# Projection of q, k and v from fp16 high and low parts in three products, with the modulation products moved in between the first row tiles

## The chip, the cores and the metric

One core of one Trainium2 chip runs the whole program. The time is the device time of one execution in microseconds (us). The engines are TensorE (PE, its weight loads PEld), VectorE (DVE), ScalarE (ACT), GpSimd (POOL) and SyncE (SP), which here only issues DMAs.

## The reference

The program is one transformer block on `x` of shape (2, 2048, 256): conditioned layer norm, attention of 16 heads, conditioned layer norm, a mixture of 8 experts. The change touches only the first part, which for each of the B = 2 batches is:

```python
mod = (silu(c) @ wmod).reshape(B, 6, 1, 256)      # rows sa, ca, ga, sb, cb, gb
ga = (2 * (ga >= 0) - 1) * max(abs(ga), 0.25)     # gb likewise
h = layernorm(x) * (1 + ca) + sa
Q, K, V = h @ Wq.T + bq, h @ Wk.T + bk, h @ Wv.T + bv
query_norms = norm(Q)                             # per row and head; the top 409 queries attend
```

## The kernel before

Two blocks of code matter, `setup_block` (L147) and `project_block` (L289). All engines run their own instruction stream and meet through semaphores; the blocks are divided by a barrier, and after the projection comes `select_block`, which starts when the rows of q and k have been written to memory.

**Setup.** Scale `1 + ca` is folded into the weights and shift `sa` into the biases. PE transposes Wq, Wv and Wk (L238), ACT copies each out of PSUM (`wt`, L209), DVE multiplies by `ca1` into `wtb` in fp32 (L280), PE computes the bias rows (L254, after two of the three copies), DVE adds them (L284).

**Projection.** There are 32 tiles of 128 rows in 8 groups of four (`BLK`); each engine runs an unrolled list of stages. In step s it runs stage number n on tile s - n, so the place in the list is the lag, and the order in the list is the order on that engine:

- DVE: `norm` (lag 0, L385, with the statistics `stats` L369 and L373 of the next group after the second tile of a group and `invert` L378 after the fourth), `evacuate` (lag 4, L396 and L397: q and v out of PSUM with their bias), `squares` (lag 5, L401), `modulation` (lag 6, L410 to L423: nine instructions in nine consecutive steps, the first for tile 5, that turn the rows `ga` and `gb` into clipped ones).
- PE: `turn_h` (lag 1, L544, two fp32 transposes), `project` (lag 3, L552, q and v at once: two fp32 products with 512 columns), `project_k` (lag 4, once in four tiles, L562: K transposed, four fp32 products with 512 columns).
- ACT: `copy_ht` (lag 2, L488, and once in a group `deviation` L482), `first` (lag 4, L495 and L497), `second` (lag 5, L501), `first_k` (lag 6, once in a group, L516 and L518 for two halves), `second_k` (lag 8, once in a group, L530).
- POOL: `second` (lag 5, L456), `third` (lag 6, L460), `second_k` (lag 7, L468), `third_k` (lag 9, L473). q and k are stored as three bf16 parts; these lines compute the rests.
- SP issues the saves of q and k (L350, L342).

An fp32 product shows in the trace as two matrix instructions, so `project` is x4 and `project_k` x8. A tile number t is passed through PSUM buffers `p_h` and `p_qv` with two copies each; `turn_h(t)` waits until the copy of tile t - 2 is out. Ahead of the first tile PE multiplies the four pieces of the modulation rows (L571, 16 matrix instructions), which ACT copies out (L535) before it does anything for a tile.

Of the kernel before, what the change touches and what calls it, by code (L numbers as in the profile page):

```python
# [16 lines left out]
F32 = mybir.dt.float32  # L17
# [8 lines left out]
P = 128  # L26
# [129 lines left out]
def setup_block(nc, ctx, io, cst):  # L156

    with ExitStack() as own:
# [19 lines left out]
        s_ps, s_done, satb_done, wt_ps, wt_done, wtb_done = sem("s_ps"), sem("s_done"), sem("satb_done"), sem("wt_ps"), sem("wt_done"), sem("wtb_done")  # L178
        bias_ps, bk_ps, bias_done = sem("bias_ps"), sem("bk_ps"), sem("bias_done")
# [4 lines left out]
        with nc.Block() as block:  # L184
# [13 lines left out]
            def _(act):  # L198
# [64 lines left out]
            def _(dve):  # L263
# [8 lines left out]
                dve.tensor_scalar(ca1[:, :, :], p_s[:, 1, :, :], 1.0, None, ALU.add).then_inc(s_done, 1)  # L272
# [3 lines left out]
                for i in range(3):  # L276
                    dve.wait_ge(wt_done, i + 1)
# [11 lines left out]
def project_block(nc, ctx, io, cst):  # L289

    with ExitStack() as own:
        sb, ps, sem = places(nc, own, "project")
        R, BLK = 4, 4
        NB = NT // BLK
# [5 lines left out]
        ht = [sb(f"ht{i}", [P, KD, BLK, P], F32) for i in range(2)]  # L300
# [15 lines left out]
        h_done, h_ps, ht_done = sem("h_done"), sem("h_ps"), sem("ht_done")  # L316
# [27 lines left out]
        with nc.Block() as block:  # L344
# [19 lines left out]
            def _(dve):  # L364
# [11 lines left out]
                def invert(j):  # L376
                    dve.wait_ge(sd_done, j + 1)
                    dve.reciprocal(rstd[j % 2][:, :], sd[j % 2][:, :]).then_inc(rstd_done, 1)  # L378

                def norm(t):  # L380

                    j, i = divmod(t, BLK)
                    wait(dve, h_ps, t - R + 1)
                    dve.wait_ge(rstd_done, j + 1)
                    dve.tensor_scalar(h[t % R][:, :], x[:, t, :], mv[j % 2][:, i, 0:1], rstd[j % 2][:, i:i + 1], ALU.subtract, ALU.mult).then_inc(h_done, 1)  # L385
                    if i == 1 and j + 1 < NB:
                        stats(j + 1)
                    if i == 3 and j + 1 < NB:
                        invert(j + 1)

                def evacuate(t):
# [4 lines left out]
                    dve.tensor_tensor(y[t % R][:, :], p_qv[t % 2][:, 0:D], biasb[:, b, 0:D], ALU.add).then_inc(y_done, 1)  # L396
                    dve.tensor_tensor(cst["v"][:, t % TPB, b, :], p_qv[t % 2][:, D:2 * D], biasb[:, b, D:2 * D], ALU.add).then_inc(v_done, 1)  # L397
# [6 lines left out]
                FIX = 5  # L404
# [22 lines left out]
                unrolled([norm, None, None, None, evacuate, squares, modulation])  # L427

                def last_keys():
# [3 lines left out]
                    dve.tensor_scalar(yk[1][:, :], p_k[1][:, :], bkb[:, 1, B - 1:B], None, ALU.add).then_inc(last_y[1], 1)  # L433
                    dve.wait_ge(k_saved[(NB - 1) % 2], 16 * KD * PARTS * ((NB - 1) // 2))
                    dve.tensor_scalar(k3[(NB - 1) % 2][1][:, 0, :], p_k[1][:, :], bkb[:, 1, B - 1:B], None, ALU.add).then_inc(last_first[1], 1)
# [42 lines left out]
            def _(act):  # L478
# [4 lines left out]

                def copy_ht(t):
# [3 lines left out]
                    act.activation(ht[t // BLK % 2][:, :, t % BLK, :], p_h[t % 2][:, 0:D].rearrange("p (k n) -> p k n", k=KD), ACT.Copy).then_inc(ht_done, 1)  # L488
# [3 lines left out]
                def first(t):  # L492
                    act.wait_ge(y_done, t + 1)
# [9 lines left out]
                def first_k(j):  # L503

                    b = j * BLK // TPB
                    if j == NB - 1:
                        act.wait_ge(k_ps, KD * j + 1)
                        act.wait_ge(krest_done, KD * (j - 1) + 1)
                        act.activation(yk[0][:, :], p_k[0][:, :], ACT.Identity, bias=bkb[:, 0, b:b + 1]).then_inc(last_y[0], 1)
                        act.wait_ge(k_saved[j % 2], 16 * KD * PARTS * (j // 2))  # L510
                        act.activation(k3[j % 2][0][:, 0, :], p_k[0][:, :], ACT.Identity, bias=bkb[:, 0, b:b + 1]).then_inc(last_first[0], 1)
# [1458 lines left out]
```

## Time and profile before

| what | value |
|---|---|
| three runs | 1243.06, 1241.56, 1240.20 us (median 1241.56) |
| the profiled execution's own time | 1228.09 us |
| its span in the trace | 1226.3 us |
| busy over the span: PE, DVE, ACT, POOL | 1008.8, 900.4, 646.7, 621.6 us |
| setup | 0 to 19.5 us |
| projection | 19.5 to 128.7 us, next block's first work at 135.0 us |

The profile is of one execution. Its times count from the start of the span. Busy is the time in which an engine runs an instruction of its own; the granted clock of PE is given as a share of full speed, 1.00 for 2.4 GHz and 0.50 for 1.2 GHz. Everything behind the projection (selection, attention, routing, experts) is the same in both kernels.

### The profile page before, as it was taken

The page shows a single profiled execution, that of the slowest core. Times are in us where ns is not written, and L with a number is a line of the kernel's source. Part 1 is how long each engine was busy: PE and PEld are TensorE (multiplying, and loading weights), DVE is VectorE, ACT ScalarE, POOL GpSimd, SP SyncE. Part 2 cuts the span into 40 slices and gives each one's busy share as a digit, 9 for nine tenths or more (in the row PEclk, how much of TensorE's full clock was granted, in tenths as well). Part 3 has the DMA queues.
Part 4 walks back from the last instruction along what each step waited for, and adds up shares of the span by engine and source line. Part 5 has one row for each costly group of instructions (what it writes and reads, how often), then busy time and mean ns, then how long its engine had stood idle before and what let it go on. Part 6 is the DMA issues. An engine that isn't in the chain of part 4 may idle for free. (4 is left out here: it accounts for less than half of the span.)

```text
span 1226.3 us, 29092 instructions
## 1 busy us (share of the span) xinstructions
PE 1008.8 (82%) x7725; PEld 616.7 (50%) x7726; DVE 900.4 (73%) x2189; ACT 646.7 (53%) x1448; POOL 621.6 (51%) x649
## 2 busy tenths in 40 slices
PE   7999002399999999999996776169999999999995
PEld 4444001133333333333333665157778888888884
DVE  4885689788777777777773887937778777777774
ACT  2778196067666666666674453335454444444441
POOL 1688382435554545554436986024554455444543
PEclk9999555589999999989998787579999999999998
DMA  6244771211111111111104895089994232223322
GB/s 222 104 148 153 258 221 60 59 28 37 33 46 31 32 44 33 44 32 32 44 4 130 251 272 172 1 213 216 232 228 79 48 52 43 47 47 52 52 43 27
DMA packets 129163, 118.69 MB, mean 97 GB/s; under 512 B 18064, under 2 KB 117072, under 8 KB 129104
## 3 DMA queue, kind: packets, MB, share of 16 engines
q1 hardware_dynamic: 106840, 95.02, 26.6%
q0 software_dynamic: 20480, 21.53, 11.0%
q10 hardware_dynamic: 1784, 1.44, 0.4%
q8 instruction: 26, 0.43, 0.2%
q14 instruction: 33, 0.27, 0.1%
HBM read 57.27 MB, written 37.60 MB: 77 GB/s over the span
## 5 line engine op out<-in xcount | busy, mean ns | idle before, releaser
L961 DVE TENSOR_REDUCE attend_mxh<-attend_p_a 128x1 f32<-128x512 f32 x416 | 266.3, 686 | 89.3 <-PE attend_p_a L1092 66.5
L1031 ACT ACTIVATE w<-attend_p_b 128x409 f32<-128x409 f32 x480 | 227.5, 514 | 128.3 <-PE attend_p_b L1108 112.4
L1832 ACT ACTIVATE expert_hr<-expert_p,b1t 128x256 f32<-128x256 f32 (+1 forms) x376 | 134.3, 423 | 192.7 <-PE expert_p L1770 138.0
L1725 POOL DMA_INDIRECT out_x<-expert_ys,expert_drop x72 | 122.3, 1699 | 190.7 <-DVE expert_ys L1867 133.5
L1108 PE MATMUL attend_p_b<-attend_qt,w 98*128 98x409 bf16 x480 | 166.9, 352 | 1.6 <-issue 1.3
L1092 PE MATMUL attend_p_a<-w,attend_qt 96*128 96x512 bf16 x384 | 153.4, 403 | 6.7 <-ACT attend_qt L1022 2.2
L905 POOL DMA_INDIRECT attn_d<-outs,idx x93 | 91.0, 978 | 118.9 <-DVE attend_mxh L961 112.5
L1792 PE MATMUL expert_p<-w,expert_hhi 128*128 x800 | 136.7, 273 | 0.6 <-DVE expert_ys L1867 0.2
L1770 PE MATMUL expert_p<-expert_xhi,w 128*128 128x256 f16 x800 | 136.3, 273 | 0.0
L886 POOL DMA_INDIRECT attend_qsel<-q_d,idx x96 | 92.2, 960 | 85.0 <-DVE attend_mxh L961 64.8
L1118 PE MATMUL attend_p_o<-w,attend_vh 128*32 128x409 f32 x1024 | 119.6, 540 | 5.9 <-ACT w L1031 3.1
L1715 POOL DMA_INDIRECT expert_xs<-h_d,expert_take x72 | 73.4, 1019 | 75.7 <-DVE expert_take L1871 54.7
L1792 PE MATMUL expert_p<-w,expert_hlo 128*128 x400 | 109.0, 273 | 0.0
L1108 PEld LDWEIGHTS attend_p_b<-attend_qt,w 98*128 98x128 bf16 x480 | 46.5, 98 | 118.6 <-ACT w L1031 79.4
L1892 DVE TENSOR_TENSOR expert_hlo<-expert_hr,expert_hhi 128x512 f16<-128x512 f32 x144 | 100.5, 698 | 5.0
L1890 DVE CAST expert_hhi<-expert_hr 128x512 f16<-128x512 f32 x144 | 62.4, 433 | 47.1 <-ACT expert_hr L1832 45.5
L1792 PEld LDWEIGHTS expert_p<-w,expert_hhi 128*128 128x128 f16 x800 | 78.2, 98 | 13.2 <-issue 3.7
L1770 PEld LDWEIGHTS expert_p<-expert_xhi,w 128*128 x800 | 78.3, 98 | 9.2
L1770 PE MATMUL expert_p<-expert_xlo,w 128*128 128x256 f16 x400 | 76.3, 273 | 0.0
L1770 PE MATMUL expert_p<-expert_xhi,expert_wu 128*128 128x128 f16 x704 | 68.2, 223 | 1.4 <-DVE expert_xlo L1875 1.4
L1787 PE MATMUL expert_p<-w,expert_hhi 128*128 x176 | 60.9, 380 | 3.1 <-issue 1.6
L1092 PEld LDWEIGHTS attend_p_a<-w,attend_qt 96*128 96x128 bf16 x384 | 38.0, 100 | 47.2 <-DVE attend_mxh L961 14.9
(352 smaller groups left out, 1955.9 us busy)
## 6 DMA issues: line engine op xcount, KB each, us to landing
expert_wu<-w SPq DMA_DIRECT2D x88, 256.0 KB
q_d<-project_q SPq DMA_DIRECT2D x32, 256.0 KB
w<-in_L_ffn_w SPq DMA_DIRECT2D x16, 512.0 KB, 4.5
route_wraw<-in_L_ffn_w SPq DMA_DIRECT2D x16, 512.0 KB, 5.0
w<-k_d SPq DMA_DIRECT2D x32, 192.0 KB
k_d<-project_k SPq DMA_DIRECT2D x45, 128.0 KB
x<-in_L_attn_x SPq DMA_DIRECT2D x8, 512.0 KB, 9.6
attn_d<-zero SPq DMA_DIRECT2D x8, 512.0 KB
```

Of the source, the lines that this page charges most:

```text
L886: pool.indirect_dma_start(out=qsel[n % U][:, c, :], out_offset=None, in_=io["q3_d"], in_offset=bass.IndirectOffsetOnAxis(ap=cst["idx"][:, ...
L905: pool.indirect_dma_start(out=io["attn_d"], out_offset=bass.IndirectOffsetOnAxis(ap=cst["idx"][:, n, c:c + 1], axis=0), in_=outs[n % 2][:, ...
L961: dve.tensor_reduce(mxh[:, c, k:k + 1], chunk_bank(a)[:, :], AX, ALU.max).then_inc(a_done, 1)
L1031: act.activation(prob[:, j, :], tile_bank(j)[:, 0:TOP], ACT.Exp, scale=SCALE).then_inc(prob_done, 1)
L1092: last = pe.matmul(into[:, :], qt[u][0:KR, c * P:(c + 1) * P], kt[u][0:KR, k * CH:(k + 1) * CH], start=True, stop=True)
L1108: pe.matmul(tile_bank(j)[:, 0:TOP], kt[u][0:KR + 2, j * P:(j + 1) * P], qt[u][0:KR + 2, 0:TOP], start=True, stop=True).then_inc(b_ps, 1)
L1118: last = pe.matmul(p_o[32 * w:32 * w + VC, 0:TOP], vh[u][:, j, :], prob[:, j, :], start=(g == 0), stop=(g == TPB // GRP - 1), tile_positio ...
L1725: pool.indirect_dma_start(out=out, out_offset=bass.IndirectOffsetOnAxis(ap=drop[u][:, s:s + 1], axis=0), in_=ys[u][:, s, :], in_offset=Non ...
L1770: last = pe.matmul(p_1[g][:, f, rows], w, xp[u][:, k, rows], start=(n == 0), stop=(n == 3 * KD - 1))
L1792: last = pe.matmul(p_2[s][:, 0:D], hp[u][:, f, s * P:(s + 1) * P], w(slice(part, part + 1)), start=(f == 0 and n == 0), stop=(f == FB - 1 ...
L1832: last = act.activation(hr[g % 2][:, f, rows], p_1[g][:, f, rows], ACT.Relu, bias=cst["b1t"][:, bass.ds(e[s] * FB + 2 * g + f, 1)], scale= ...
L1892: dve.tensor_tensor(hlo[u][:, 2 * g:2 * g + 2, :], hr[g % 2][:, :, :], hhi[u][:, 2 * g:2 * g + 2, :], ALU.subtract).then_inc(hlo_done, 1)
```

## The change

The weights `wtb` are scaled by 256 (`WSCALE`) and kept as two fp16 parts, high and low; the transposed rows likewise (`hthi`, `htlo`). Each product becomes three fp16 products, high times high, high times low and low times high; the results are divided by 256 where they are taken out of PSUM. ACT now makes the high parts (in setup and in `copy_ht`), DVE the low parts. `norm` is written as x times rstd plus shift, even tiles on DVE and odd ones on ACT. The modulation products and their copies follow tiles 1, 2, 4 and 5 in `project` and `first`, and `modulation` on DVE starts a step later.

```diff
@@ setup_block, ACT and DVE
+                    act.wait_ge(s_done, 2)
+                    act.wait_ge(wt_done, i + 1)
+                    for b in range(B):
+                        for k in range(KD):
+                            act.activation(cst["wtb"][:, b, k, 0, i * D:(i + 1) * D], wt[:, k, i * D:(i + 1) * D], ACT.Copy, scale=ca1[:, k, b:b + 1]).then_inc(whi_done, 1)
...
-                            dve.tensor_scalar(cst["wtb"][:, b, k, i * D:(i + 1) * D], wt[:, k, i * D:(i + 1) * D], ca1[:, k, b:b + 1], None, ALU.mult)
+                            dve.wait_ge(whi_done, (i * B + b) * KD + k + 1)
+                            dve.scalar_tensor_tensor(out=cst["wtb"][:, b, k, 1, i * D:(i + 1) * D], in0=wt[:, k, i * D:(i + 1) * D], scalar=ca1[:, k, b:b + 1],
+                                                     in1=cst["wtb"][:, b, k, 0, i * D:(i + 1) * D], op0=ALU.mult, op1=ALU.subtract)
@@ project_block, DVE
+        MOD_AT = (1, 2, 4, 5)
...
                     dve.reciprocal(rstd[j % 2][:, :], sd[j % 2][:, :]).then_inc(rstd_done, 1)
+                    dve.wait_ge(rstd_done, j + 1)
+                    dve.scalar_tensor_tensor(out=shift[j % 2][:, :], in0=mv[j % 2][:, :, 0], scalar=-1.0, in1=rstd[j % 2][:, :], op0=ALU.mult, op1=ALU.mult).then_inc(shift_done, 1)
...
-                    dve.tensor_scalar(h[t % R][:, :], x[:, t, :], mv[j % 2][:, i, 0:1], rstd[j % 2][:, i:i + 1], ALU.subtract, ALU.mult).then_inc(h_done, 1)
+                    if t % 2 == 0:
+                        dve.tensor_scalar(h[t % R][:, :], x[:, t, :], rstd[j % 2][:, i:i + 1], shift[j % 2][:, i:i + 1], ALU.mult, ALU.add).then_inc(h_done[0], 1)
...
+                def low(t):
+                    dve.wait_ge(hthi_done, t + 1)
+                    at = lambda a: a[t // BLK % 2][:, :, t % BLK, :]
+                    dve.tensor_tensor(at(htlo), p_h[t % 2][:, 0:D].rearrange("p (k n) -> p k n", k=KD), at(hthi), ALU.subtract).then_inc(htlo_done, 1)
...
-                unrolled([norm, None, None, None, evacuate, squares, modulation])
+                for step in range(NT + 6):
+                    for lag, stage in ((0, norm), (4, evacuate), (2, low), (5, squares), (6, modulation)):
@@ project_block, ACT
+                def norm(t):
+                    if t % 2:
+                        act.activation(h[t % R][:, :], x[:, t, :], ACT.Identity, scale=rstd[j % 2][:, i:i + 1], bias=shift[j % 2][:, i:i + 1]).then_inc(h_done[1], 1)
...
                 def first(t):
+                    if t in MOD_AT:
+                        i = MOD_AT.index(t)
+                        act.wait_ge(mod_ps, i + 1)
+                        act.activation(mod[:, i // 2, (i % 2) * 512:(i % 2 + 1) * 512], p_mod[i % 2][:, :], ACT.Copy).then_inc(mod_done, 1)
...
-                unrolled([None, None, copy_ht, None, first, second, last_of_block(first_k), None, last_of_block(second_k)])
+                unrolled([norm, None, copy_ht, None, first, second, last_of_block(first_k), None, last_of_block(second_k)])
@@ project_block, PE
-                    wait(pe, ht_done, t - 1)
+                    wait(pe, htlo_done, t - 1)
...
-                    for k in range(KD):
-                        last = pe.matmul(p_qv[t % 2][:, :], ht[t // BLK % 2][:, k, t % BLK, :], wtb[:, t // TPB, k, 0:2 * D], start=(k == 0), stop=(k == KD - 1))
+                    for n, (hp, part) in enumerate(((hthi, 0), (hthi, 1), (htlo, 0))):
+                        for k in range(KD):
+                            last = pe.matmul(p_qv[t % 2][:, :], hp[t // BLK % 2][:, k, t % BLK, :], wtb[:, t // TPB, k, part, 0:2 * D],
+                                             start=(n == 0 and k == 0), stop=(n == 2 and k == KD - 1))
                     last.then_inc(qv_ps, 1)
+                    if t in MOD_AT:
+                        modulation(MOD_AT.index(t))
```

`project_k` gets the same loop over three products. `evacuate` and the copies of K take a factor 1/256 in the instruction that adds the bias; their number stays the same.

## Rows read from the trace of the kernel before

**Rows 1.** Window, its length, busy PE, PEld, DVE, ACT, POOL; granted clock, DMA share, GB/s
```profile
44.60:117.10 72.50, 68.23 (x192) 30.94 (x191) 55.40 (x139) 56.22 (x138) 61.29 (x73) 1.00 0.43 146
```
**Rows 2.** Timeline of PE: start, duration, instruction, count; two group periods' K products
```profile
72.10 0.41 PE L544 MATMUL project_p_h<-ident,project_h 128*128 128x128 f32 x2 [1.31 <-ACT project_ht L488]
...
72.34 1.88 PE L552 MATMUL project_p_qv<-wtb,project_ht 128*128 128x512 f32 x4
74.06 3.60 PE L562 MATMUL project_p_k<-project_ht,wtb 128*128 128x512 f32 x8
77.50 0.38 PE L544 MATMUL project_p_h<-ident,project_h 128*128 128x128 f32 x2
...
86.03 3.60 PE L562 MATMUL project_p_k<-project_ht,wtb 128*128 128x512 f32 x8
```
**Rows 3.** Timeline of ACT: first K copy of groups 0 and 6, and one group between
```profile
44.63 0.67 ACT L516 ACTIVATE project_yk<-project_p_k,bkb 128x512 f32<-128x512 f32 x1
...
80.09 0.63 ACT L495 ACTIVATE project_q<-project_y 128x512 bf16<-128x512 f32 x1 [1.79 <-DVE project_y L396]
80.63 0.40 ACT L497 ACTIVATE project_sq<-project_y 128x256 f32<-128x256 f32 x1
...
81.24 0.67 ACT L516 ACTIVATE project_yk<-project_p_k,bkb 128x512 f32<-128x512 f32 x1
...
83.52 0.39 ACT L488 ACTIVATE project_ht<-project_p_h 128x256 f32<-128x256 f32 x1
...
83.97 0.65 ACT L495 ACTIVATE project_q<-project_y 128x512 bf16<-128x512 f32 x1
...
86.50 1.16 ACT L530 ACTIVATE project_k<-project_krest 128x512 bf16<-128x512 f32 x2
87.54 0.40 ACT L488 ACTIVATE project_ht<-project_p_h 128x256 f32<-128x256 f32 x1
...
117.14 0.67 ACT L516 ACTIVATE project_yk<-project_p_k,bkb 128x512 f32<-128x512 f32 x1
```
**Rows 4.** Timeline of DVE: statistics of a group ahead of the next evacuation
```profile
77.37 1.39 DVE L369 BATCH_NORM_STATS2 project_st<-x 128x6 f32<-128x256 f32 x4
78.80 0.38 DVE L373 BATCH_NORM_AGGREGATE project_mv<-project_st 128x2 f32<-128x6 f32 x4
79.64 0.42 DVE L396 TENSOR_TENSOR project_y<-project_p_qv,biasb 128x256 f32<-128x256 f32 x1 [0.46 <-PE project_p_qv L552]
79.98 0.41 DVE L397 TENSOR_TENSOR v<-project_p_qv,biasb 128x256 f32<-128x256 f32 x1
```
**Rows 5.** Timeline of PE in the attention stage: a 16-bit product with 512 columns
```profile
301.18 0.38 PE L1092 MATMUL attend_p_a<-w,attend_qt 96*128 96x512 bf16 x1
...
301.40 0.34 PE L1108 MATMUL attend_p_b<-attend_qt,w 98*128 98x409 bf16 x1
```
**Rows 6.** Timeline of setup's end and of the projection's first work
```profile
12.14 0.60 ACT L209 ACTIVATE setup_wt<-setup_p_w 128x512 f32<-128x512 f32 x1 [5.81 <-PE setup_p_w L238]
...
19.58 7.10 PE L571 MATMUL project_p_mod<-wmod,silub 128*128 128x512 f32 x16 [1.03 <-PEq L80]
...
21.98 0.73 DVE L385 TENSOR_SCALAR project_h<-x,project_mv,project_rstd 128x256 f32<-128x256 f32 x2
```
**Rows 7.** Groups by line and shape, 0 to 130 us: two of the modulation instructions
```profile
L423 DVE SCALAR_TENSOR_TENSOR mod<-project_mag,project_sgn 128x512 f32<-128x512 f32 x2 | 1.5, 730 | 0.0
...
L410 DVE TENSOR_SCALAR mod<-mod 128x512 f32<-128x512 f32 x1 | 0.6, 569 | 0.0
```
**Rows 8.** Windows of 1 us: PE's busy time and granted clock after idle time
```profile
122.00:123.00 1.00, 0.36 (x1) 0.00 (x0) 0.60 (x1) 1.00 (x3) 1.00 (x3) 1.00 0.05 18
...
124.00:125.00 1.00, 0.00 (x0) 0.00 (x0) 0.00 (x0) 0.41 (x1) 1.00 (x2) 0.77 0.68 262
...
366.00:367.00 1.00, 1.00 (x9) 0.94 (x10) 0.94 (x2) 0.74 (x2) 0.95 (x1) 0.94 0.00 0
...
373.00:374.00 1.00, 1.00 (x7) 0.16 (x9) 0.82 (x2) 0.69 (x2) 0.00 (x0) 0.65 0.00 0
```

More of the change, by code:

```diff
@@ L299, in project_block @@
         h = [sb(f"h{i}", [P, D], F32) for i in range(R)]
-        ht = [sb(f"ht{i}", [P, KD, BLK, P], F32) for i in range(2)]
+        hthi = [sb(f"hthi{i}", [P, KD, BLK, P], F16) for i in range(2)]
+        htlo = [sb(f"htlo{i}", [P, KD, BLK, P], F16) for i in range(2)]
+        shift = [sb(f"shift{i}", [P, BLK], F32) for i in range(2)]
         y = [sb(f"y{i}", [P, D], F32) for i in range(R)]
@@ L315, in project_block @@
         mod_ps, mod_done, signs, sizes, centred, fixed = sem("mod_ps"), sem("mod_done"), sem("signs"), sem("sizes"), sem("centred"), sem("fixed")
[L316 removed]
+        h_done, h_ps, hthi_done, htlo_done = [sem(f"h_done{i}") for i in range(2)], sem("h_ps"), sem("hthi_done"), sem("htlo_done")
+        shift_done = sem("shift_done")
         qv_ps, y_done, v_done, part0_done, sq_done = sem("qv_ps"), sem("y_done"), sem("v_done"), sem("part0_done"), sem("sq_done")
@@ L403, in _ @@
                 row = lambda j: mod[:, :, j * D:(j + 1) * D]
-                FIX = 5
+                FIX = 6
                 def modulation(t):
@@ L426, in _ @@
                 invert(0)
-                unrolled([norm, None, None, None, evacuate, squares, modulation])
+                for step in range(NT + 6):
+                    for lag, stage in ((0, norm), (4, evacuate), (2, low), (5, squares), (6, modulation)):
+                        if 0 <= step - lag < NT:
+                            stage(step - lag)
                 def last_keys():
@@ L532, in _ @@
                 deviation(0)
-                for i in range(4):
-                    act.wait_ge(mod_ps, i + 1)
-                    act.activation(mod[:, i // 2, (i % 2) * 512:(i % 2 + 1) * 512], p_mod[i % 2][:, :], ACT.Copy).then_inc(mod_done, 1)
-                unrolled([None, None, copy_ht, None, first, second, last_of_block(first_k), None, last_of_block(second_k)])
+                unrolled([norm, None, copy_ht, None, first, second, last_of_block(first_k), None, last_of_block(second_k)])
             @block.tensor
@@ L560, in project_k, with modulation @@
                         wait(pe, yk_done, KD * (j - 1) + oc + 1)
-                        for k in range(KD):
-                            last = pe.matmul(p_k[oc][:, :], wtb[:, b, k, 2 * D + oc * P:2 * D + (oc + 1) * P], ht[j % 2][:, k, :, :].rearrange("p t n -> p (t n)"),
-                                             start=(k == 0), stop=(k == KD - 1))
+                        for n, (hp, part) in enumerate(((hthi, 0), (hthi, 1), (htlo, 0))):
+                            for k in range(KD):
+                                last = pe.matmul(p_k[oc][:, :], wtb[:, b, k, part, 2 * D + oc * P:2 * D + (oc + 1) * P], hp[j % 2][:, k, :, :].rearrange("p t n -> p (t n)"),
+                                                 start=(n == 0 and k == 0), stop=(n == 2 and k == KD - 1))
                         last.then_inc(k_ps, 1)
-                pe.wait_ge(cst["rows_here"], 16)
-                for i in range(4):
+                def modulation(i):
+                    if i == 0:
+                        pe.wait_ge(cst["rows_here"], 16)
                     b, c = divmod(i, 2)
```

36 lines of the change are left out of this document (20 added, 16 removed).

## The prediction

> **What bounds the kernel now.** I first read the busy time by window. Between the first K copy on ACT and the seventh, six groups of four tiles, PE is busy 68.2 of 72.5 us, POOL 61.3, ACT 56.2 and DVE 55.4 [rows 1]: PE sets the pace, but POOL and ACT are at 85% and 78% of it. PE's timeline then gives the prices. Start to start, `turn_h` takes 0.24 us, `project` 1.72 (x4 at 0.43), `project_k` 3.44, so a group needs 4 x 1.96 + 3.44 = 11.3 us of PE; it recurs every 11.97 us in the middle [rows 2], and every 12.08 on average, (117.14 - 44.63) / 6, over the seven first K copies [rows 3]. So a faster PE can win only until the next engine or chain binds, and that is what I work out.
>
> **PE's work per group.** An fp16 product with 512 columns is bounded by the 16-bit one of 512 columns in the attention stage, 0.22 us start to start [rows 5]. Six per tile: 1.30; twelve for K: 2.6. A group: 4 x (0.24 + 1.30) + 2.6 = 8.8 us instead of 11.3. The weight loads double in number per fp32 product but lie beside the products.
>
> **ACT's own work.** Start to start in the group shown: square and `second` 0.61 together (80.63 to 81.24), `first`'s copy 0.54, `copy_ht` with `deviation` 0.45 once, 0.27 without, `first_k` 2.28 (81.24 to 83.52), `second_k` 1.04 [rows 3]. A group: 4 x (0.27 + 0.54 + 0.61) + 0.18 + 2.28 + 1.04 = 9.2. The change adds two `norm`, which I bound from below by the square's pace of 0.31 and from above by 0.50 and take as 0.35 (same shape, same source): 9.9 us. POOL keeps its work, 61.3 / 6 = 10.2 at most, part of it waiting on the port it shares with DVE. Neither is under 9.9, so 12.08 can't fall below some 10.
>
> **The chain that I expect to bind.** `low` on DVE stands between the evacuation and the next statistics, and it waits for `copy_ht` of the same step on ACT. Count time from the end of ACT's `first_k` (0). ACT then does one step (copy 0.27, deviation 0.18, 0.54, 0.61: to 1.60), one with `norm` and `second_k` (2.81: to 4.41), and copies the next rows out (ready at 4.81). DVE can only now run `low` and `squares` (0.34 apart, as L396 and L397 are [rows 4], to 5.5), then the group's statistics: from their start to the end of the aggregation is 1.81 us [rows 4], so the evacuation comes at 7.3 and q is ready at 7.73. ACT, free for it since 4.41 + 0.27 + 1.15 + 0.35 + 0.27 = 6.45, waits 1.3 us, and then needs 0.54 + 0.61 + 2.28 to end `first_k`. Period: 11.2 us. Before, the same statistics were hidden, because the evacuation behind them waited another 0.46 us for PE anyway [rows 4]. Bounds: 9.9 if the wait vanishes, 12 if `norm` on ACT, port waits and semaphores add up to 0.8.
>
> **Modulation on DVE.** With `FIX` at 6, three of its instructions (0.57 and twice 0.73 [rows 7]) fall into the step whose DVE work ends in that chain: + 2.0 us in all; the group average before has its own share in 12.08. Six groups: 6 x 11.2 + 2.0 = 69.2 instead of 72.5, **-3.3 us**.
>
> **Setup.** ACT now puts four high parts between its first and second copy of weights. They can start at 11.4 us (`sat` ready) and take 4 x 0.35, so the second copy starts at 12.9 instead of 12.14 [rows 6], and with it the bias products that end setup: + 0.8 us (bounds 0.4 and 1.6). The low parts on DVE, 12 instead of 12, wait for ACT but end before the bias sum that follows; if they don't, the same half microsecond is lost once.
>
> **The first tiles.** Before, the 16 modulation products hold PE from 19.58 for 7.1 us, and tile 0 waits for them: its `norm` starts at 21.98 already [rows 6]. After: 0.8 later and behind the shift (0.2), so `norm(0)` runs from 23.0 to 23.4. Then DVE does the statistics of group 1 (1.8), `norm(2)` and only then `low(0)`, to 25.8; `project(0)` ends at 27.1. From there to the end of tile 5 with its modulation products PE is the bound: five steps of 1.54 (7.7), 16 modulation products at 0.43 (6.9) and the first K products (2.6): 17.2, to 44.3. ACT copies the fourth modulation piece (0.55), then `first`, square and `second`: first K copy at 46.0. That is 1.4 us later than before, although tile 0 starts earlier: the modulation products are moved in between the tiles, not removed, and PE is still the bound there.
>
> To this comes PE's clock. After setup PE has nothing for about 4 us (19.5 to 23.5) and little until 25.8. In the trace, after its last product at 122.4 the granted clock fell to 1.2 GHz within the window of 124 to 125, and in the attention stage it fell in the window at 366 and came back in the one at 373, with PE busy throughout [rows 8]. The steps up to tile 2 then run at half speed. That stretch at half speed was some 7 us long; I take 5.6, since PE is less busy here at first but the fall may come late; it costs 2.8 (bounds 0 and 4). Before, the modulation products filled just this hole. The Trainium skill, "TensorE: Matmul & The Clock Gate", Part 1, says the same in general: idleness throttles the array to half rate and activity releases it. Without such a fall the first K copy is at 46.0, with it at 48.8: **+ 4.2 us** against 44.63.
>
> **The end.** From the last full `first_k` on, POOL's rests and ACT's copies of the last groups set the end in both kernels, at the same distance; + 0. The saves (DMA share 0.43 [rows 1]) keep their order and have room. Selection and all behind it is unchanged and starts when the saves have landed.
>
> **Sum.** + 4.2 - 3.3 = + 0.9 us. The profiled execution takes 1228.09 us itself, so 1229.0; its span is 1226.3, and the median of the three runs is 1241.56, 1.1% above it. I carry the difference over in microseconds: **1242.5 us**. About 0.2%, 2.5 us, is what a measurement can tell from no change. This case's own range is 1238.5 to 1246.5: 0 to 4 for the clock, +/- 2 for six periods, +/- 0.6 for setup. Chance 0.36.
>
> **Rivals.**
> - *The chain does not bind, ACT's work does.* If DVE runs ahead (for instance because `copy_ht` comes out of ACT's queue sooner than I count), the period is ACT's 9.9 plus some 0.5 of small waits, 10.4: 6 x (12.08 - 10.4) = 10.1 won; with the modulation instructions hidden, + 4.2 - 10.1 = - 5.9, 1235.7; without the early clock loss - 8.7, 1232.9. For it: DVE's own work in a group (16 instructions 0.34 apart, two `norm`, 1.81, some 0.5 to invert: 8.5) is under ACT's. Against: the order within the queues, which sets the chain whatever the totals are. A smaller form, where only the clock stays up at the start, gives 1.4 - 3.3 = - 1.9. Together 0.29.
> - *The clock falls in every group (slower).* In my schedule PE has, ahead of the step with the K products, only 1.5 us of work in 4.2, with a last gap of 2.2 us. Before, the gap was 1.3 [rows 2] and the clock stayed at 1.00 [rows 1]. If it now falls each time, the 5.6 us of PE work behind it (K step and the next tile) run partly at half speed; 3 to 4 us at half cost 1.5 to 2, of which the chain's slack takes up 1.0, so the period is 11.9 and more: - 1 or + 1 for six groups instead of - 3.3, and about + 5 to + 7 in all with the start, 1247 to 1249. It decides from the point where the gap ends in a fall in more than about half of the groups. By the Trainium skill's rule on idle gaps (the same page, "HAM oscillation") this is the case to fear; the rows here show a fall after a gap of some 2.4 us [rows 8] and none after 1.3. Chance 0.25.
> - *Port waits on ACT's or POOL's side take the stall's place.* POOL at 10.2 of 11.2 us delays `second`, ACT waits for the rest: 0.1 to 0.3 per group, 1243 to 1245. Chance 0.06.
> - *The products are not cheaper.* Should the alternation of parts cost the products more than 0.22 us each, PE stays at about 11 and nothing is won: + 4.2 less 0 to 1, 1244.8 to 1246. The 16-bit pace [rows 5] speaks against it. Chance 0.04.
>
> **How the numbers follow.** Faster by over 0.2%: 0.29, the first rival. Within it: 0.32 of the forecast's case and 0.05 of the port case, 0.37. Slower: 0.25 for the clock in every group, 0.04 for dear products, 0.05 for the upper ends of the other two, 0.34. The range 1234 to 1249 takes in nearly all but the far end of the first rival and of the second.
>
> **What would show it.** First K copy of ACT at 48 to 50 us, the seventh at 117 to 119; a granted clock of 0.50 in some windows between 22 and 32; PE's share in the middle windows down to about 78% with a clock of 1.00; and ACT's longest waits for `project_y` once a group, behind DVE's statistics. The forecast is wrong if the K copies recur at 10.5 us or less, or if the middle windows show clocks of 0.5.

## The result, and the profile after

| what | before | after |
|---|---|---|
| median (range) of 20 runs each | 1237.85 us (1230.96 to 1243.56) | 1247.54 us (1240.79 to 1250.16) |
| ratio after / before | | 1.0075, 95% interval 1.0059 to 1.0091 |
| profiled execution: its time, its span | 1228.09, 1226.3 us | 1248.91, 1247.1 us |
| statistics of the first group start (DVE) | 19.58 | 22.05 |
| first K copies of ACT: first, seventh | 44.63, 117.14 | 50.69, 123.80 |
| selection's first product (PE) | 135.06 | 141.60 |

The change made the kernel slower by 0.75%, some 9 us. The projection ends 6.5 us later: 6.06 us are lost up to the first K copy, and six groups of four tiles take 73.1 us instead of 72.5, although PE's work in them fell. Of the rest of the 21 us between the two spans, 14.2 lie in the attention stage, whose code is the same. These are its windows, before and after:

```profile
233.00:657.20 424.20, 399.71 (x2816) 140.28 (x2816) 311.78 (x708) 276.31 (x609) 204.71 (x234) 0.94 0.14 32
239.20:677.60 438.40, 409.07 (x2817) 141.58 (x2818) 312.19 (x708) 276.98 (x609) 204.63 (x235) 0.92 0.13 31
```

PE's clock is lower there after the change, 0.92 instead of 0.94. Part of it is the choice of the profiled execution: that of before, 1228.09 us, is faster than each of the 20 runs of its kernel. Whether another part belongs to the change isn't shown. One chip of the later runs takes about 1240 us as well; there the stage took 434.3 to 438.8 us in four traces, all of changed kernels, and the kernel before was not profiled. On faster chips it took 388.8 to 392.6 us, with the kernel before (389.2) as with changed ones.

PE was relieved. This is the window over the same six groups, with the clock's windows at the start and in one group; columns as in [rows 1]:

```profile
50.60:123.80 73.20, 58.70 (x265) 27.23 (x263) 56.80 (x158) 61.43 (x150) 61.20 (x73) 0.93 0.41 141
...
22.00:28.00 6.00, 1.55 (x6) 1.14 (x7) 5.20 (x24) 3.62 (x7) 0.00 (x0) 0.57 0.09 28
28.00:33.00 5.00, 5.00 (x15) 2.10 (x13) 2.83 (x9) 2.08 (x5) 0.67 (x1) 0.50 0.01 2
...
69.00:70.00 1.00, 1.00 (x4) 0.41 (x3) 1.00 (x3) 1.00 (x4) 1.00 (x2) 0.50 0.62 240
```

PE is busy for 58.7 us instead of 68.2 [rows 1], though part of that at half rate: the clock is 0.93 on the mean. ACT rose from 56.2 to 61.4. No engine is over 84%, which points to a chain across engines. PE's timeline of one group, against [rows 2]:

```profile
77.26 0.59 PE L586 MATMUL project_p_qv<-wtb,project_htlo 128*128 128x512 f16 x2
79.81 0.41 PE L577 MATMUL project_p_h<-ident,project_h 128*128 128x128 f32 x2 [1.95 <-DVE project_htlo L409]
80.05 1.07 PE L586 MATMUL project_p_qv<-wtb,project_hthi 128*128 128x512 f16 x4
...
81.77 1.91 PE L600 MATMUL project_p_k<-project_hthi,wtb 128*128 128x512 f16 x4
83.47 1.02 PE L600 MATMUL project_p_k<-project_htlo,wtb 128*128 128x512 f16 x2
84.33 1.03 PE L600 MATMUL project_p_k<-project_hthi,wtb 128*128 128x512 f16 x4
...
85.84 1.03 PE L586 MATMUL project_p_qv<-wtb,project_hthi 128*128 128x512 f16 x4
86.70 0.59 PE L586 MATMUL project_p_qv<-wtb,project_htlo 128*128 128x512 f16 x2
87.14 0.38 PE L577 MATMUL project_p_h<-ident,project_h 128*128 128x128 f32 x2
```

At full rate six fp16 products take 1.30 us (85.84 to 87.14), as reckoned. At 79.81 PE has waited 1.95 us; some 1.1 us later its rate halves (four K products from 81.77 take 1.70 us instead of 0.86) and comes back at 84.3. ACT's timeline, against [rows 3]:

```profile
50.69 0.68 ACT L552 ACTIVATE project_yk<-project_p_k,bkb 128x512 f32<-128x512 f32 x1
...
76.53 0.67 ACT L552 ACTIVATE project_yk<-project_p_k,bkb 128x512 f32<-128x512 f32 x1
...
85.53 0.58 ACT L514 ACTIVATE project_h<-x,project_shift,project_rstd 128x256 f32<-128x256 f32 x1
86.04 0.39 ACT L520 ACTIVATE project_hthi<-project_p_h 128x256 f16<-128x256 f32 x1
88.77 0.63 ACT L531 ACTIVATE project_q<-project_y 128x512 bf16<-128x512 f32 x1 [2.34 <-DVE project_y L416]
...
89.92 0.67 ACT L552 ACTIVATE project_yk<-project_p_k,bkb 128x512 f32<-128x512 f32 x1
...
123.80 0.67 ACT L552 ACTIVATE project_yk<-project_p_k,bkb 128x512 f32<-128x512 f32 x1
```

The seven first copies stand at 50.69, 63.13, 76.53, 89.92, 102.33, 113.06 and 123.80: periods of 12.44, 13.40, 13.39, 12.41, 10.73 and 10.74. ACT's longest wait of the group shown, 2.34 us, is for `project_y`, where the prediction had it. DVE's timeline shows what stands ahead of that evacuation, against [rows 4] and [rows 7]:

```profile
79.90 0.86 DVE L436 SCALAR_TENSOR_TENSOR project_mag<-mod 128x512 f32<-128x512 f32 x1
...
84.93 0.40 DVE L421 TENSOR_REDUCE nrm<-project_sq 128x16 f32<-128x256 f32 x1
85.26 1.44 DVE L443 SCALAR_TENSOR_TENSOR mod<-project_mag,project_sgn 128x512 f32<-128x512 f32 x1
86.62 1.39 DVE L380 BATCH_NORM_STATS2 project_st<-x 128x6 f32<-128x256 f32 x4
...
88.34 0.39 DVE L416 SCALAR_TENSOR_TENSOR project_y<-project_p_qv,biasb 128x256 f32<-128x256 f32 x1
```

POOL works at the same time; these two of its instructions run until 0.55 us ahead of the end of the one of 1.44 us:

```profile
83.83 2.32 POOL L497 TENSOR_TENSOR project_k<-project_krest,project_k 128x512 bf16<-128x512 f32 x2
```

The product for the evacuation at 88.34 was ready at 87.3 (PE, 86.70 and 0.59): it waits behind a modulation instruction and the statistics. Setup and the first tiles, from the timeline, against [rows 6]:

```profile
11.34 1.71 ACT L215 ACTIVATE wtb<-setup_wt,setup_ca 128x256 f16<-128x256 f32 x4 [5.22 <-DVE setup_sat L279]
12.96 0.57 ACT L210 ACTIVATE setup_wt<-setup_p_w 128x512 f32<-128x512 f32 x1
...
13.67 6.55 PE L260 MATMUL setup_p_bias<-setup_wt,setup_satb 128*128 128x512 f32 x8 [0.82 <-ACT setup_wt L210]
...
22.05 1.41 DVE L380 BATCH_NORM_STATS2 project_st<-x 128x6 f32<-128x256 f32 x4 [0.84 <-PEq L80]
...
25.11 1.12 PE L577 MATMUL project_p_h<-ident,project_h 128*128 128x128 f32 x4 [4.11 <-DVE project_h L400]
...
33.35 1.88 PE L610 MATMUL project_p_mod<-wmod,silub 128*128 128x512 f32 x4
```

Four high parts hold ACT's second copy back to 12.96. PE then idles 4.1 us ahead of 25.11, and its clock is at half from 23 to 33, until just ahead of the first modulation product. Last, the waits between 44 and 130 us (engine, line, waited for; total, times, longest):

```profile
PE project_p_h L577 <- DVE project_htlo L409: 14.5, 9, 1.9
DVE project_htlo L409 <- ACT project_hthi L520: 12.5, 14, 2.1
ACT project_q L531 <- DVE project_y L416: 11.1, 10, 2.4
```

I read them as one loop: PE waits for DVE's low part, DVE for ACT's high part, ACT for DVE's evacuation.

### The profile page after: what moved, and what is told of

It is laid out like the page before. It is cut to its first block and busy times, and to the rows that moved or that the text cites. A ratio compares the mean times of both kernels' runs of the same rounds, so it can differ in the third digit from the quotient of the medians.

```text
span 1247.1 us, 29345 instructions
## 1 busy us (share of the span) xinstructions
PE 1008.1 (81%) x7821; PEld 612.3 (49%) x7822; DVE 905.5 (73%) x2213; ACT 659.7 (53%) x1476; POOL 621.6 (50%) x649
## 3 DMA queue, kind: packets, MB, share of 16 engines
q10 hardware_dynamic: 1784, 1.44, 0.4%
## 5 line engine op out<-in xcount | busy, mean ns | idle before, releaser
L1148 PE MATMUL attend_p_b<-attend_qt,w 98*128 98x409 bf16 x480 | 170.8, 359 | 2.4 <-issue 1.6
L1132 PE MATMUL attend_p_a<-w,attend_qt 96*128 96x512 bf16 x384 | 156.3, 410 | 12.2 <-ACT attend_qt L1062 8.5
```

The lines of the kernel that those rows point to most:

```text
L1132: last = pe.matmul(into[:, :], qt[u][0:KR, c * P:(c + 1) * P], kt[u][0:KR, k * CH:(k + 1) * CH], start=True, stop=True)
L1148: pe.matmul(tile_bank(j)[:, 0:TOP], kt[u][0:KR + 2, j * P:(j + 1) * P], qt[u][0:KR + 2, 0:TOP], start=True, stop=True).then_inc(b_ps, 1)
```

## The experiments

Each run is compared by its ratio to the kernel before on the same chip, and by the places of the K copies, whose distances agreed from chip to chip where the edit left them alone. There were four chips. The kernel before takes 1238 us on one of them (`c_after`, `e4_setup_split`, `e7_ahead_gap`, `e8_all`) and 1193 to 1194 on the other three; there `e1_mod_ahead`, `e2_keep_warm`, `e3_no_mod_dve` and `e5_stats_late` ran on the first, `c_before`, `e9_ahead_full` and `e10_two_ahead` on the second, `e11_no_fill` on the third. My theory: chain of 11.2 us per group, plus modulation instructions in that chain, plus a start lost to the hole behind setup. The rivals: the clock falling in the groups, or ACT's and the port's own work.

**The two kernels again.** The kernel after (`c_after`) and the kernel before (`c_before`), unchanged.

> The changed kernel itself, once more, on the chip of the other runs and beside them. Theory A (everything it loses lies ahead of the selection): the projection ends 6.5 us later than before's trace has it, with K copies at the same places to 0.3 us, and the whole is 6 to 7 us (0.5 to 0.6%) longer than the kernel before. Rival B (the later start shifts the attention stage into a worse pattern of the clock and costs more there): 9 us (0.75%) or more here too, with the same places in the projection.

> The kernel before, profiled once more, to see how much of the difference behind the projection is the execution's own. Theory A (the attention stage varies between executions and chips by more than the change moves it): the projection's K copies at the places of the first trace to 0.5 us, and the attention stage within 5 us of the changed kernel's on the same chip. Rival B (the changed kernel lengthens the attention stage by its shifted start): attention some 13 us shorter than the changed kernel's, as in the first pair of traces.

After: 1245.98 us, ratio 1.0059 [1.0036, 1.0083]; statistics at 20.68, first K copy at 48.70 (2 us earlier than expected), periods as above, selection at 139.27. Before: 20.16, 45.21 and 135.64, one execution, 1193.24 us. It ran on one of the faster chips, so it says nothing of my two theories on the attention stage. The start of one and the same kernel moves by 2 us from execution to execution, and the difference in the projection's end is 3.6 to 6.5 us.

**Modulation products ahead of the tiles again**, with the rest of the change kept.

```diff
-                    if t in MOD_AT:
-                        modulation(MOD_AT.index(t))
...
+                for i in range(4):
+                    modulation(i)
                 unrolled([None, turn_h, None, project, last_of_block(project_k)])
```

> The changed kernel, with the four modulation products and their copies put back ahead of the first tile. Theory A (the moved products leave PE without work after setup, its clock falls, and then they lie on PE's critical path between the first tiles): the clock stays at 1.00 from 22 us on, tile 0 starts some 2 us later, but the first K copy on ACT comes at 44 to 46 us instead of 50.7, and the whole is 4 to 6 us shorter than the changed kernel. Rival B (the place of the modulation products does not matter, since the later groups bind): first K copy still at 49 to 51, or the seventh no earlier than 123, and the time within 2 us of the changed kernel's 1247.5.

Ratio 1.0009 [0.9994, 1.0023]. From the windows and the timelines of ACT and PE:

```profile
30.00:124.00 94.00, 71.87 (x350) 34.55 (x350) 74.75 (x215) 78.92 (x194) 72.78 (x89) 1.00 0.38 132
```
```profile
46.40 0.67 ACT L548 ACTIVATE project_yk<-project_p_k,bkb 128x512 f32<-128x512 f32 x1
...
58.83 0.67 ACT L548 ACTIVATE project_yk<-project_p_k,bkb 128x512 f32<-128x512 f32 x1
72.22 0.67 ACT L548 ACTIVATE project_yk<-project_p_k,bkb 128x512 f32<-128x512 f32 x1
```
```profile
71.85 0.41 PE L576 MATMUL project_p_h<-ident,project_h 128*128 128x128 f32 x2 [2.42 <-DVE project_htlo L409]
...
75.50 0.41 PE L576 MATMUL project_p_h<-ident,project_h 128*128 128x128 f32 x2 [1.95 <-DVE project_htlo L409]
```

From the statistics' start (22.27) to the first K copy it takes 24.1 us; the kernel after takes 28.6 and 28.0 in its two traces, the kernel before 25.05 in both. Moving the modulation products between the tiles therefore costs about 4 us. That is the place of the products and the fall of the clock that comes with it; no run holds the clock up with the products in between, so the two aren't told apart. The selection starts at 135.54, where before has it (135.06, 135.64). The clock stayed at 1.00, though PE waits as long in the groups as in the kernel after and longer (2.42). Yet the next three periods are 12.43, 13.39 and 13.40, the same as with the clock falling; only the fourth is shorter, 11.18 instead of 12.41.

**PE kept busy in the groups**: unread fp16 products behind the third and fourth tile of each group.

```diff
+                    if 7 <= t < NT - 1:
+                        for _ in range({2: 3, 3: 8}.get(t % BLK, 0)):
+                            pe.matmul(p_mod[0][:, :], wtb[:, 0, 0, 0, 0:P], wtb[:, 0, 0, 0, 0:2 * D], start=True, stop=True)
```

> The changed kernel with extra fp16 products on PE whose result nobody reads: three after the third tile of a group and eight after the fourth, from tile 7 on, into a PSUM bank that is free by then; they fill the gaps in which PE waits for the low parts. Theory A (the clock falls in those gaps and costs the group behind them): the granted clock stays at 1.00 from 50 to 125 us, the groups that recur at 13.4 and 12.4 us now do so at 12.4 and 10.7, and the seventh K copy comes 4 to 5 us earlier, near 119.5, though PE does more. Rival B (the clock falls beside work that waits anyway; the DVE and ACT chain sets the period): periods unchanged at 12.4 to 13.4, nothing won, or lost by the extra products.

Ratio 1.0039 [1.0021, 1.0057]. The clock is 1.00 from 36 us on, the periods 12.43, 13.40, 13.40, 11.18, 10.73, 11.02: a held clock wins 1.2 us, in group 4 alone, and the unread products cost 0.3 in the last. Falls in the groups aren't the cause of the three long periods.

**DVE's nine modulation instructions left out** (the clipping of the rows `ga` and `gb` isn't done).

```diff
-                    for lag, stage in (..., (5, squares), (6, modulation)):
+                    for lag, stage in (..., (5, squares)):
```

> The changed kernel without the nine DVE instructions that turn the modulation rows into clipped ones (so the rows used later are the unclipped ones). Theory A (three of them per group stand in the chain from DVE's low part to the next evacuation): the second K copy comes 10.7 us after the first instead of 12.4, the third and fourth 12.4 or less instead of 13.4, and the seventh 4 to 5 us earlier in all. Rival B (they fill DVE's idle time): periods unchanged to 0.3 us; the long periods are the clock's alone.

Periods 11.19, 11.18, 12.42, 11.19, 12.41, 10.73; one execution, 1192.39 us. The second of them on ACT and DVE:

```profile
59.80 0.67 ACT L552 ACTIVATE project_yk<-project_p_k,bkb 128x512 f32<-128x512 f32 x1
...
69.83 0.63 ACT L531 ACTIVATE project_q<-project_y 128x512 bf16<-128x512 f32 x1 [0.97 <-DVE project_y L416]
...
70.98 0.67 ACT L552 ACTIVATE project_yk<-project_p_k,bkb 128x512 f32<-128x512 f32 x1
```
```profile
67.35 0.41 DVE L421 TENSOR_REDUCE nrm<-project_sq 128x16 f32<-128x256 f32 x1
67.68 1.40 DVE L380 BATCH_NORM_STATS2 project_st<-x 128x6 f32<-128x256 f32 x4
...
69.41 0.39 DVE L416 SCALAR_TENSOR_TENSOR project_y<-project_p_qv,biasb 128x256 f32<-128x256 f32 x1
```

This is the predicted chain with its length, 11.18. ACT's wait is 0.97 (I had 1.3). In the two periods of 12.4 the clock falls, so a fall costs 1.2 us where no modulation instruction covers it. The instructions themselves cost 12.43 - 11.18, 13.39 - 11.18 and 13.40 - 11.18 (periods of `e1_mod_ahead`, whose clock holds): 5.7 us.

**Statistics behind `low`**, so that they leave the chain.

```diff
-                    if i == 1 and j + 1 < NB:
-                        stats(j + 1)
...
+                        if stage is low and step % BLK == 1 and step // BLK + 1 < NB:
+                            stats(step // BLK + 1)
```

> The changed kernel with the statistics of the next group moved on DVE from ahead of the evacuation to behind the low part of the same step. Theory A (the statistics stand in the binding chain): the warm period falls from 10.73 to 10.2 or 10.4, what ACT's own instructions need, ACT's wait for q ahead of its K copies (0.5 to 2.3 us once a group) is gone, and PE's gap gets shorter, so that the clock falls less often; the seventh K copy 3 to 7 us earlier. Rival B (ACT alone or POOL binds): the warm period stays at 10.7.

A miss: one execution, 1204.63 us; periods 10.74, 14.24, 14.16, 12.96, 12.97, 10.72. In DVE's and PE's timeline of the third:

```profile
76.27 1.38 DVE L432 TENSOR_SCALAR project_sgn<-mod 128x512 f32<-128x512 f32 x1
77.58 1.24 DVE L400 TENSOR_SCALAR project_h<-x,project_rstd,project_shift 128x256 f32<-128x256 f32 x1
```
```profile
79.95 0.66 PE L577 MATMUL project_p_h<-ident,project_h 128*128 128x128 f32 x2 [3.73 <-DVE project_htlo L407]
```

The statistics now delay the next evacuation and `low` instead, and `norm` lasts 1.24 us instead of 0.41, beside a POOL instruction of 1.29 us that started at 77.38. PE's gap grows to 3.73 us. The clock fell in four of these groups.

**Setup's high parts split**: two of them ahead of ACT's remaining copies, ten behind.

```diff
+                copy_out(0)
+                for piece in pieces[:2]:
+                    high(*piece)
+                copy_out(1)
+                copy_out(2)
+                for piece in pieces[2:]:
+                    high(*piece)
```

> The changed kernel with setup reordered: on ACT two high parts, then the second and third copy of weights, then the other ten; on DVE the first bias sum ahead of the last four low parts. Theory A (the four high parts between the first and the second copy held back the bias products, and with them the clock): bias products start at 12.9 instead of 13.7, reach full pace some 2 us earlier, the projection's first instruction comes 1.5 to 2.2 us earlier, and so does the first K copy. Rival B (setup ends with ACT's and DVE's own parts): the projection starts within 0.5 us of the changed kernel's 22.0.

Statistics at 20.21, but first K copy only at 49.07 (48.70 in `c_after` on the same chip); one execution, 1248.42 us. The clock fell at 21.5 and stayed down for 10 us. What setup gives, the hole behind it takes.

**The parts together.** Four kernels, each the kernel after with: modulation products ahead and DVE's nine instructions moved, two per group from step 14 on, into DVE's own waits (`e7_ahead_gap`); this with late statistics, setup split and unread products (`e8_all`); `e7` with setup split, unread products in the groups and three more at setup's end (`e9_ahead_full`); and that with only two modulation products ahead, two behind tiles 4 and 5 (`e10_two_ahead`).

```diff
-                    for lag, stage in (..., (5, squares), (6, modulation)):
+                    for lag, stage in (..., (5, squares)):
+                        if stage is low and step % BLK == 2 and step >= 14:
+                            for n in (0, 1):
+                                modulation(FIX + 2 * (step - 14) // BLK + n)
```

> Modulation products ahead of the first tile, and DVE's nine modulation instructions moved into the steps in which it waits for ACT's high part, two in each, ahead of the low part. Theory A (their place in the chain costs 1.2 and twice 2.2 us, not their work): K copies recur at 11.2 us from the first on, 10.7 in the last two groups, 1.2 more where the clock falls; first K copy at 46.4, seventh at 112.6 to 115, 2 to 4.5 us ahead of the kernel before, ratio 0.997 to 0.999. Rival B (DVE's total work counts, or the waits they fill are not there): periods of 12.4 and more remain and the seventh comes at 117 or later.

Ratio 0.9983 [0.9956, 1.0009]. Periods 11.18, 11.18, 11.19, 12.56 (a fall of the clock), 10.86, 10.74; first K copy at 45.64. The modulation instructions are hidden (the first two last 0.41 us each there): six periods take 67.7 us, where the prediction has 67.2 for the chain alone. The ratio isn't told apart from 1.

> All that should help together: modulation products ahead, modulation instructions in DVE's waits, statistics behind the low part, setup reordered, and unread fp16 products in PE's gaps to hold the clock. Theory A (chain and clock both cost, and are removed together): clock 1.00 throughout, periods of 10.7 or less in every group, first K copy at 44 to 45, seventh at 108.5 to 109.5, 8 us ahead of the kernel before, ratio about 0.9935. Rival B (ACT and POOL together can't keep 10.7 over all groups, or the extra products delay PE's own): periods over 11.2, seventh K copy at 112 or later, ratio 0.996 or more.

A miss again: 1.0012 [0.9988, 1.0036], periods 11.28, 12.72, 13.00, 12.98, 12.99, 11.02, though the unread products held the clock at 1.00 in these groups. So late statistics are bad by their place on DVE, and the fall of the clock doesn't explain `e5_stats_late`. DVE there:

```profile
82.75 1.39 DVE L392 BATCH_NORM_STATS2 project_st<-x 128x6 f32<-128x256 f32 x4
...
84.78 1.26 DVE L412 TENSOR_SCALAR project_h<-x,project_rstd,project_shift 128x256 f32<-128x256 f32 x1
...
86.62 0.98 DVE L453 SCALAR_TENSOR_TENSOR mod<-project_mag,project_sgn 128x512 f32<-128x512 f32 x1
```

> Modulation products ahead, modulation instructions in DVE's waits, statistics at their old place, setup reordered with three unread fp32 products at its end, and unread fp16 products in the gaps of the groups. Theory A: clock 1.00 throughout, first K copy at 43.5 to 44.5, four periods of 11.2 and two of 10.7, the seventh at 110 to 111, 6 us ahead of the kernel before: ratio 0.995. Rival B (the extra products or the reordered setup cost what they save): first K copy at 45.6 or later or periods over 11.4; ratio 0.998 or more.

Ratio 0.9994 [0.9979, 1.0008]. Periods right (11.18 to 11.19 four times, then 10.88 and 11.01), start missed: first K copy at 47.64; the three products at setup's end take 2.8 us and delay the barrier. The time is missed too: selection starts at 131.74, 3.9 us ahead of before on that chip, but the ratio gives 0.7 us.

> As the run with everything ahead, but two modulation products ahead and two after tiles 4 and 5. Theory A (ahead of tile 0 PE has a hole of some 4 us, so only what does not fit into it costs): first K copy 1 us earlier than with all four ahead, near 43, since tile 0 no longer waits, and the rest the same. Rival B (the two products after tiles 4 and 5 lie on PE's path and ACT waits for them): first K copy no earlier, or later by up to 3 us.

Ratio 0.9958 [0.9944, 0.9972], 1188.89 against 1193.97 us: this beats the kernel before, and by the ratios (1.0075 and 1.0059) the kernel after. First K copy at 46.71, selection at 130.79, 0.9 and 1.0 us earlier than with four products ahead; the whole is 4.5 us shorter, and where the rest of that lies isn't shown.

**The same without the three products at setup's end.**

```diff
-                for _ in range(3):
-                    pe.matmul(p_w[0][:, :], satb[:, 0, 0, :], wt[:, 0, 0:2 * D], start=True, stop=True)
```

> As the kernel with two modulation products ahead, but without the three unread fp32 products at setup's end, which there took 2.8 us of PE and held the barrier back (statistics start at 22.73 instead of some 20.2 to 21.0). Theory (they only delay; the two modulation products start right behind setup and keep the clock up by themselves): first K copy 1.5 to 2.5 us earlier, 44.2 to 45.2, periods 11.2 x4, selection at 128.5 to 129.5, ratio to the kernel before 0.993 to 0.995. Rival (the bias products end setup at half rate, or the clock falls in the shorter work behind setup): a granted clock of 0.50 in windows between 20 and 32, first K copy at 46.5 or later, ratio 0.996 or more.

Ratio 0.9962 [0.9945, 0.9980], 1189.40 against 1193.27 us. PE's and ACT's timeline and the window over six groups:

```profile
20.52 3.67 PE L642 MATMUL project_p_mod<-wmod,silub 128*128 128x512 f32 x8 [1.18 <-PEq L80]
24.03 0.60 PE L604 MATMUL project_p_h<-ident,project_h 128*128 128x128 f32 x4
```
```profile
44.50 0.68 ACT L567 ACTIVATE project_yk<-project_p_k,bkb 128x512 f32<-128x512 f32 x1
...
111.16 0.67 ACT L567 ACTIVATE project_yk<-project_p_k,bkb 128x512 f32<-128x512 f32 x1
```
```profile
44.50:111.20 66.70, 66.38 (x327) 32.55 (x326) 54.88 (x158) 60.82 (x150) 59.59 (x73) 1.00 0.45 156
```

Two modulation products fit into the hole that the statistics leave: tile 0 is turned 0.5 us later behind `norm` than in the kernel after, but its low part starts 4.95 us behind the statistics in both, and the clock stays at 1.00. The projection ends 6.7 us earlier than in the second trace of before (128.95 against 135.64, two of the faster chips), as the theory had it. The ratio was expected at 0.993 to 0.995 and missed: a gain of 4.5 us against 5.0 with the three products, with intervals that overlap. Whether the 2.2 us that the trace shows reach the time isn't settled.

## Why the prediction was right and wrong

The measured 1247.5 us lies in the range of 1234 to 1249, 5 us over the predicted 1242.5 and outside the case's own 1238.5 to 1246.5. That is luck in part: the sum started from 1241.56, the median of three runs, and over 20 runs the median is 1237.85. From there the same + 0.9 gives 1238.8, and the range's upper end 1245.3. The change itself was missed: "within 0.2%" had the largest chance (0.37), and "slower" (0.34) came. The sum had + 0.9 us where the projection's end moved by + 6.5, or by 3.6 and 4.2 if the second trace of after is set against the two of before. By the prediction's own signs the forecast failed: middle windows show a clock of 0.50, and the seventh K copy stands at 123.8 (121.8 in the second trace), not at 117 to 119.

- **PE's work and what bounds behind it: right.** fp16 products at 0.22 us; PE's share fell to 80%, and the chain through DVE's statistics binds at 11.18 to 11.19 us where nothing else is in it; predicted 11.2. Rival 1 (the chain doesn't bind) is out: the period is 10.73 only in the last two, which hold no statistics any more (the last group's start at 97.80). That I had not foreseen; it gave back 0.9 us. What sets 10.73 isn't shown: ACT is busy for 19.8 of the 21.5 us, but still waits 0.5 and 1.2 for `project_y`. The small pieces were off in both directions: `norm` on ACT is 0.49 apart and not 0.35, the wait 0.97 and not 1.3.
- **Modulation on DVE: the step that failed.** "2.0 us in all" was 5.7. I took the durations of [rows 7] and let three of nine instructions count. All of the first three groups pay: 1.25, 2.2 and 2.2. The nine last 0.78 to 1.44 us; before, they lasted 0.53 to 1.15. In each of the three groups one stands directly ahead of the statistics, and these three last 1.33, 1.44 and 1.44. They start while POOL runs the two instructions of L497 and end only 0.3 to 0.55 us behind them (the second ends at 86.15, DVE's at 86.70). [rows 7] have 0.73 for the same instruction, where POOL had only 0.2 us left at its start; alone it lasts 0.68 (`e7_ahead_gap`). In group 3 the one of 1.44 costs 1.36 us from start to start. The other 0.85 is lost earlier: the sum ahead of it (L421) starts 8.40 us behind the K copy, in `e3_no_mod_dve` 7.55. So the others count too. Moved into DVE's waits the nine cost nothing: the first three periods of `e7_ahead_gap` are 33.55 us, against 39.23.
- **The groups: - 3.3 predicted, + 0.6 measured.** The sum's 69.2, with 3.7 more for modulation, 1.2 for the clock in group 4 and 0.9 less in the last two, makes 73.2; 73.1 were measured.
- **Behind setup: right in size.** 25.05 us from statistics to the first K copy before, 28.6 and 28.0 after, + 3.0 to 3.6; the sum had 4.2 - 0.8 = 3.4, with the clock's 2.8 in it. In the trace the clock was down for 10 us, but PE had little to do in half of it. `e1_mod_ahead` takes all of this away (24.1). How much of it is the clock's stays open; with the clock down for 7 us instead of 10 (`c_after`) it is 0.6 us less.
- **Setup: + 0.8 predicted, + 2.5 and + 1.1 measured** against 19.58. The copy moved by 0.82 as reckoned. The rest is in how late PE reaches its full rate: the bias products come 0.85 us apart at first and 0.43 later, and the eight take 6.55 us in one execution and 5.30 in the other (before 4.87 and 5.57). Where full rate comes at nearly the same place, at 16.8 us in `c_after` and 16.6 in `c_before`, the statistics start 0.5 us later after the change and the selection 3.6. So that pair is the fairer one, and some 3 of the first pair's 6.5 us come with the later full rate. Seven traces with this setup have full rate at 16.8 to 19.8 us; whether the edit has a part in that isn't shown.
- **Rival 2, the clock in every group: seen but not as priced.** It falls in groups 2 to 4, behind gaps of 1.95 us, not in 1, 5 and 6 with gaps of 1.90 to 1.93. It costs 1.2 us where the chain is exposed and nothing where modulation binds anyway (`e2_keep_warm`: periods unchanged). Its 1247 to 1249 was hit, but by other terms, and does not follow from its own: - 1 or + 1 for the groups and + 4.2 for the start give 1244.8 to 1246.8. The Trainium skill, "TensorE: Matmul & The Clock Gate", "HAM oscillation", advises to keep idle gaps out so that the array stays at full rate. Its rule is written for longer gaps than these, so it doesn't foresee the falls at 1.95 us. The runs agree that the clock holds with the gaps filled (1.00), but it also held with gaps of 2.42 us in `e1_mod_ahead`, and it is worth little while another chain binds.

The later end of the projection thus has two causes, shown by taking each away: the modulation products moved out of a hole that PE has anyway (4 us, the clock's fall included), and modulation instructions in DVE's exposed chain (5.7 us against 2.0 expected), which eat the gain of the cheaper products. What stays open: the first measurement gives at least + 7.3 us (the repeat at least + 4.5), and the fairer pair of traces + 3.6 for the projection. No stage that the change touches shows the rest. The attention stage may hold it: on the chip of 1238 us it took 438.2 us in `c_after` and 434.3 in `e7_ahead_gap`, each profiled within 0.2 us of its kernel's median. A trace of before on that chip would tell, and there is none.

## What to carry to other kernels

When a change relieves the engine that bounds, write out the chain that binds next and place every instruction of side work (here nine on DVE) against it, at its duration beside the neighbours that it will have, not at its duration before. Side work belongs into a wait that exists: two modulation products in PE's hole behind setup held nothing back, four cost 0.9 us more (`e9_ahead_full` against `e10_two_ahead`), and with none the clock fell. Unread products to hold the clock pay only where the clock is in the binding chain: here 1.2 us in one group, less 0.3 in the last. And a forecast of a difference is worth no more than the base that it is added to: three runs were 3.7 us off.

## What the runs showed of the hardware

- In setup PE runs at half rate for a while, and the windows don't show it. They read 1.00 from 3 to 22 us in the trace of after, but the fp32 products with 512 columns come 0.85 us apart (two per microsecond from 14 to 18). In the trace of before they are 0.85 us apart until 14.7 and 0.43 from 15.5 on, and its first record of the granted clock stands at 15.31 us: ahead of it a window's 1.00 means no record. In all 14 traces the spacing halves at the first record, if there are products left behind it; it stands between 14.4 and 19.8 us and moves by 2.6 between two executions of one kernel.
- The length of a gap doesn't decide alone whether the clock falls. In the kernel after it fell behind gaps of 1.95 us in groups 2 to 4 and not behind 1.93, 1.90 and 1.90 in the others, in both traces. In `e1_mod_ahead` PE has gaps of 1.90 to 2.42 us in all six groups and the clock stays at 1.00; in `e7_ahead_gap` six of 1.90 to 2.09 and one fall. What decides isn't shown. A fall lasts about 3 us and costs the period 1.2 where the chain is exposed.
- A DVE instruction of this kernel that works from SBUF alone and starts beside a running POOL instruction ends only behind it, so its length goes by what POOL has left. `norm` on 256 columns ends some 0.15 us behind POOL's end: 0.66 us beside one of 0.67, 1.24 beside one of 1.29 (`e5_stats_late`), against 0.41 alone. Of the modulation instructions, tensor_scalar on 512 columns ends 0.28 us behind it and scalar_tensor_tensor 0.55, the same in both kernels; so the latter lasts 0.73 us in one place [rows 7], 1.44 in another and 0.68 with no POOL instruction running at its start (`e7_ahead_gap`). The batch statistics kept their 1.39 us for four beside POOL.
- An ACT instruction with a scale and a bias per partition lasts 0.60 us (0.49 to the next) where copies of 256 columns last 0.40 (0.27). The Trainium skill, "ScalarE: Activation LUTs", "What ACT_TABLE_LOAD costs", gives 93 ns for each such operand; by it 0.40 becomes an estimated 0.59, which the trace agrees with.
- The attention stage, the same code in all kernels, follows the clock that a chip grants: 424.2 to 438.8 us at 0.92 to 0.94 in six traces on the chips that take about 1240 us, 388.8 to 392.6 on the faster chips (0.97 in `c_before`).
